# A perceiver block on one core: six of eight softmax normalisations on GpSimd, the output product in two halves of heads, and routing one-hots made one strip earlier

## The reference, cut to what matters

```python
x = x + xattn(layernorm(x), ctx, ctx)     # x: 64 x 64 x 256, ctx: 64 x 256 x 256
x = x + attn(layernorm(x))                # self attention with rotary positions
out = x + ffn(layernorm(x))               # shared expert, and top 2 of 8 routed experts

def xattn(query, key, value):             # 16 heads of 64
    q, k, v = query @ Wq + bq, key @ Wk + bk, value @ Wv + bv
    attn = softmax(q k^T / 8)             # per batch and head 64 x 256
    out = (attn v) @ Wo + bo + query      # 1024 -> 256
    return (out - mean) * rsqrt(var + 1e-5) * gamma + beta
```

## Time and profile before

| | us |
|---|---|
| three timed runs | 2184.82, 2184.95, 2186.15 |
| their median | 2184.95 |
| the profiled execution | 2187.32 |
| span of its trace (first to last instruction) | 2185.6 |
| PE busy | 2117.3 |
| DVE busy | 1609.6 |
| ACT busy | 1280.6 |
| POOL busy | 675.7 |
| cross attention | from the start to about 1407 |
| shared expert's sixteen strips with placing | 1717 to 1800 |

### The profile page before, as it was taken

One profiled execution on the slowest core, in us unless ns is written; L12 is line 12 of the kernel. 1 busy time (PEld: TensorE's weight loads), 2 busy tenths in 40 slices (PEclk: granted clock), 3 DMA queues, 4 the chain that ended last, 5 costly groups with the idle time before them and its releaser, 6 DMA issues.

```text
span 2185.6 us, 46111 instructions
## 1 busy us (share of the span) xinstructions
PE 2117.3 (97%) x15864; PEld 1855.5 (85%) x15865; DVE 1609.6 (74%) x3025; ACT 1280.6 (59%) x3067; POOL 675.7 (31%) x620
## 2 busy tenths in 40 slices
PE   8999999999999999999999999899998999999997
PEld 7898888888888888888888888677776888888886
DVE  6667768778777677687687786699996767666665
ACT  5556566556566565566565665477775335555553
POOL 4011011011010010110110101188885234777775
PEclk9999999999999999999999999999999999999999
DMA  4001010010010010010100100244433222333332
GB/s 153 10 21 34 0 34 24 10 34 19 14 34 19 15 34 14 19 32 2 34 24 10 34 10 1 63 153 153 151 121 100 87 78 51 54 55 53 53 55 42
DMA packets 100685, 103.90 MB, mean 48 GB/s; under 512 B 11952, under 2 KB 90160, under 8 KB 100624
## 3 DMA queue, kind: packets, MB, share of 16 engines
q1 hardware_dynamic: 86992, 84.47, 12.4%
q0 software_dynamic: 13632, 18.62, 5.2%
HBM read 72.52 MB, written 30.54 MB: 47 GB/s over the span
## 4 chain that ended last, share of the span: by engine, by line
PE 56%; DVE 17%; issue 10%; POOL 10%; ACT 4%; DMA 2%; DVEq 1%; POOLq 0%; SPq 0%; ACTq 0%
PE banks L906 29%; PE banks L949 5%; PE banks L991 5%; PE banks L1001 5%; POOL out_dram L2378 4%; PE banks L976 4%; POOL r_x L2342 3%; PE banks L2217 3%; DVE q_st L652 2%; POOL index L2349 2%; DVE s_peak L1535 2%; DVE s_rsum L1581 2%; ACT probs L541 2%; DVE z L846 1%; DMA out_dram<-r_y,index 1%
## 5 line engine op out<-in xcount | busy, mean ns | idle before, releaser
L906 PE MATMUL banks<-ctxT_hi,qk_hi 128*128 128x256 f32 x1024 | 300.5, 293 | 0.0
L906 PE MATMUL banks<-ctxT_hi,qk_lo 128*128 128x256 f32 x1024 | 289.5, 283 | 0.0
L906 PE MATMUL banks<-ctxT_lo,qk_hi 128*128 128x256 f32 x1024 | 288.4, 282 | 0.0
L541 ACT ACTIVATE probs<-banks,nbias 128x256 f32<-128x256 f32 x512 | 236.6, 485 | 71.6 <-DVE nbias L674 71.2
L548 ACT ACTIVATE pc<-banks 128x512 f32<-128x512 f32 x256 | 153.0, 598 | 191.3 <-PE banks L906 186.5
L632 DVE TENSOR_TENSOR qk_lo<-banks,qk_hi 128x512 fp32r<-128x512 f32 x256 | 165.8, 685 | 68.9 <-ACT qk_hi L503 68.8
L906 PE MATMUL banks<-pT_hi,ctx_hi 128*128 128x512 f32 x512 | 206.2, 403 | 4.7 <-DVE qk_lo L632 3.1
L432 POOL TENSOR_TENSOR rstd<-mv,power 128x2 f32<-128x2 f32 x32 | 22.2, 694 | 597.0 <-DVE mv L724 597.0
L632 DVE TENSOR_TENSOR pT_lo<-banks,pT_hi 128x512 fp32r<-128x512 f32 x256 | 164.6, 684 | 56.3 <-ACT pT_hi L503 55.7
L906 PE MATMUL banks<-pT_hi,ctx_lo 128*128 128x512 f32 x512 | 201.6, 394 | 0.0
L906 PE MATMUL banks<-pT_lo,ctx_hi 128*128 128x512 f32 x512 | 200.2, 391 | 0.0
(11 more groups left out here) (271 smaller groups left out, 6062.4 us busy)
## 6 DMA issues: line engine op xcount, KB each, us to landing
ctx_raw<-in_ctx_dram SPq DMA_DIRECT2D x64, 256.0 KB, 2.7
experts_w<-in_L_ffn_We_dram SPq DMA_DIRECT2D x24, 512.0 KB, 4.0
x_in<-in_x_dram SPq DMA_DIRECT2D x16, 256.0 KB, 2.8
x_again<-in_x_dram SPq DMA_DIRECT2D x16, 256.0 KB, 2.9
x_stream<-z SPq DMA_DIRECT2D x16, 256.0 KB, 2.2
s_x<-x_stream SPq DMA_DIRECT2D x32, 128.0 KB, 3.7
s_x_again<-x_stream SPq DMA_DIRECT2D x32, 128.0 KB, 2.1
x_normalised<-s_xl SPq DMA_DIRECT2D x32, 128.0 KB, 1.7
```

The source lines that it names most:

```text
L541: nc.scalar.activation(probs[:, s % 2, p, :], scores[:, s % 2, p // 2, (p % 2) * SK:(p % 2 + 1) * SK], ACT.Exp, bias=nbias[:, s % 2, p:p + ...
L906: last = nc.tensor.matmul(out, a, b, start=(n == 0), stop=(n == 3 * len(pairs) - 1))
```

## The change

Three edits.

1. Normalising of steps 1 to 6 moves to GpSimd: a power of -1 of the four sums (`rinv`), then the product of 128x1024. Steps 0 and 7 stay on DVE. GpSimd's program is rewritten by steps, and the context tiles 2 and 3 are now split in steps 0 and 1 of the group that uses them, behind the normalising of step 1 for the last one.
2. The output product is made by halves of the heads instead of by tiles. The bank of half 1 (four pairs, both tiles) is made in step 7 of the same group and added to `resid`; that of half 0 in step 3 of the next, and added to give `z`. The number of matmuls is the same: eight in each bank. In step 3 the first `do_pc` bank comes behind the second fold instead of the fourth. In step 7 DVE does `peaks` first, then `ctx_lower`.
3. `spread_out` is done one strip earlier.

```diff
-def part_of_pc(half, i):
-    c = i - (1 if half else 2)
+def part_of_pc(i):
+    c = i - 1
...
-                if s == 3 and g.prev and i < TILES:
-                    out.append(("o", i))
+                if i == 0 and (g.cur if half else g.prev):
+                    out.append(("o", half))
...
+        def normalise(g, s):                       # GpSimd
+            pool.wait_ge(exp_done, PAIRS * (STEPS * g.at + s + 1))
+            pool.sem_inc(pool_past, 1)
+            nc.gpsimd.tensor_tensor(rinv[:, s % 2, :], rsum[:, s % 2, :], inverse[:, :], ALU.pow).then_inc(rinv_done, 1)
+            pool.wait_ge(rinv_done, len(POOL_STEPS) * g.at + s)
+            pool.sem_inc(pool_past, 1)
+            nc.gpsimd.tensor_tensor(probs[:, s % 2], probs[:, s % 2],
+                                    rinv[:, s % 2, :].unsqueeze(2).broadcast_to([P, PAIRS, SK]),
+                                    ALU.mult).then_inc(probs_pool, 1)
...
+            for s in range(STEPS):
+                if s == 4 and g.prev:
+                    rsqrt(g, 1, tail_stats, tail_rstd, g.at)
+                if s == 4 and g.next:
+                    rsqrt(g, 0, ln_stats, ln_rstd, g.at + 2)
+                if s in POOL_STEPS:                # 1 to 6
+                    normalise(g, s)
+                if s < 2 and g.prev:
+                    split_ctx(g, s + 2, -1)
+                if s >= 6 and g.next:
+                    split_ctx(g, s - 6)
...
+        def add_o(g, half, out):                   # DVE
+            bank, free = wait_filled(dve, g, ("o", half))
+            nc.vector.tensor_tensor(out[:, :, :], bank.rearrange("p (n d) -> p n d", n=TILES), resid[:, :, :],
+                                    ALU.add).then_inc(free, 1)
...
-                if s == STEPS - 1 and g.next:
-                    ctx_lower(g, b)
-                    for h in range(2):
-                        fold_lower(g, half, h)
                 if g.cur:
                     peaks(g, s)
-                if half == 1 and g.next and s < STEPS - 1:
+                if half == 1 and g.next:
                     ctx_lower(g, b)
...
-                if g.cur:
+                if g.cur and s not in POOL_STEPS:
                     normalise(g, s)
...
         def do_pT(g, s):
-            pe.wait_ge(probs_done, STEPS * g.at + s)
+            if s - 1 in POOL_STEPS:
+                pe.wait_ge(probs_pool, len(POOL_STEPS) * g.at + s - 1)
+            else:
+                pe.wait_ge(probs_done, 2 * g.at + s)
...
-        def do_o(g, n):
+        def do_o(g, half):
             for j in range(2):
-                wait_freed(pe, g, ("v", 0, j))
-            bank, done = bank_for(pe, g, ("o", n))
-            for m in range(HALF):
-                last = nc.tensor.matmul(bank[:, 0:D], oT[:, m, n * P:(n + 1) * P], wo[:, m, :],
-                                        start=(m == 0), stop=(m == HALF - 1))
+                wait_freed(pe, g, ("v", half, j))
+            bank, done = bank_for(pe, g, ("o", half))
+            first = (1 - half) * PAIRS
+            for n in range(TILES):
+                for m in range(first, first + PAIRS):
+                    last = nc.tensor.matmul(bank[:, n * D:(n + 1) * D], oT[:, m, n * P:(n + 1) * P], wo[:, m, :],
+                                            start=(m == first), stop=(m == first + PAIRS - 1))
             last.then_inc(done, 1)
...
-            if 0 <= i + 1 - PLACE_AT < BATCHES:
-                spread_out(i + 1 - PLACE_AT)
+            if 0 <= i + 2 - PLACE_AT < BATCHES:
+                spread_out(i + 2 - PLACE_AT)
```

More of the change, by code:

```diff
@@ L831, in vector @@
                 if b == 3:
-                    for i in range(half, HALF // 2):
-                        if s == 3 and g.prev and i < TILES:
-                            bank, free = wait_filled(dve, g, ("o", i))
-                            nc.vector.tensor_tensor(z[:, i, :], bank[:, 0:D], resid[:, i, :], ALU.add).then_inc(free, 1)
+                    for i in range(HALF // 2):
+                        if s == 7 and g.cur and i == 0:
+                            dve.wait_ge(resid_done, g.at + 1)
+                            add_o(g, half, resid)
+                        if s == 3 and g.prev and i == 0:
+                            wait_freed(dve, g, ("o", 1), -1)
+                            add_o(g, half, z)
                         if s == 7 and g.next and i == 3:
```

60 lines of the change are left out of this document (23 added, 37 removed).

## The result

| | before | after |
|---|---|---|
| median of the runs, us | 2184.89 (2184.11 to 2186.15, 4 runs) | 2171.73 (2170.11 to 2173.67, 4 runs) |
| span of the profiled execution, us | 2185.6 | 2170.1 |
| granted clock of TensorE | 0.994 | 0.993 |

The ratio is 0.9936, with a 95% interval of 0.9924 to 0.9949: faster by 0.51 to 0.76%. The forecast was 2169.0 us, which is 15.9 us less; measured are 13.2 us less.

What follows compares the result with a forecast made beforehand. Only TensorE was full, so the change could give only its stalls. Terms summed to -16.0 us: 2187.3 to 2171.3 us for the profiled execution, 2169.0 for the median (2.4 lower); own range 2163 to 2176.

Steps and rivals of the forecast that it cites:

- placing: Sixteen placings and the wait before the first: with one-hots a strip earlier the losses go, -4.8 us, bounds -5.2 and -3.
- the block: DVE operations reading two SBUF tiles wait for GpSimd's product; `top` in steps 2, 5 and 6 takes 1 to 1.5 us.
- step 6: Step 6 of a group: `nbias` and `xT_lower` half a microsecond later, just in time; 0.05 x 15 = +0.8 us.
- first and last group: First group: -0.9 at the wait for DVE's first fold, +0.3 in step 2; last group's moved output product costs the same.
- step 7, folds: TensorE's 0.9 us lost at step 7's folds all goes behind the output product; -0.9 x 15 = -13.5 us.
- step 3, folds: Folds 4 to 7 in a row make TensorE wait at the last two banks; 0.38 x 15 = +5.7 us.
- step 5, transposes: Second bank of transposes gets back 0.33 of 0.59 us lost, since `top` waits for POOL's product; -5.0 us.
- step 2, exponentials: `top` held up, exponentials 0.8 us later, queries and second transposes bank 0.1 late; 14 groups, +1.4 us.
- `nbias` behind cast and subtraction: Rival: in step 2 POOL's cast and subtraction both precede `nbias`, 1.4 us instead of 0.1; 2187 us, chance 0.11.
- the slow neighbour: Rival: POOL's product takes 2427 ns instead of 1907, delaying steps 2, 5 and 6; 2190.5 us, chance 0.12.
- No block: Rival: small operations slip in, step 5 gives 0.59 us, steps 2 and 6 cost nothing; 2163 us, chance 0.14.
- Stalls elsewhere: Rival: the six losses of 0.1 us return in the new order, step 7 gains only 0.29; 2178 us, chance 0.13.

Runs made afterwards that it cites:

- halves_dve: The changed kernel with all eight normalisations of a group on DVE, new order kept; 2170.63 us, ratio 0.9938 to the kernel before.
- pc_apart: The changed kernel with step 3's two `do_pc` banks behind the folds of slots 0 and 2 instead of 0 and 1; 2170.55 us, ratio 0.9942.
- output_between: The changed kernel with step 3's output half between the folds of slots 0 and 1, `do_pc` behind slots 1 and 2; 2172.17 us, ratio 0.9939.
- nbias_on_act: The changed kernel with the exponentials' bias made by ScalarE, VectorE left with the maximum alone; 2163.57 us, ratio 0.9902.
- act_all: act_rec4 plus the step 3 order of output_between; 2160.50 us, ratio 0.9885.
- act_rec4: nbias_on_act plus, in step 4 alone, the reciprocal on DVE behind the residual additions; 2157.99 us, ratio 0.9872.

## Why the prediction was right, point by point

The time was 2.7 us off. The mechanisms held where the large terms are: the losses that go in step 7 and at the placings, the block in steps 2 and 5, the new loss in step 3. The small terms (step 6, first and last group) did not come as put, and the placings are right in sum with some luck, as told below. Between the spans of the two profiled executions lie 15.5 us, close to the 16.0 of the sum; that is luck too, since 4.0 of them are in the start, which is not the change's. The medians differ by 13.2: the profiled execution lay 2.4 us above the median before and 0.1 above it after. The measured terms are read from the steps:

| term | predicted | measured | by |
|---|---|---|---|
| step 7, folds | -13.5 | -13.0 | -(13.15 - 15.60 + 3.38), x 14 |
| step 3, folds | +5.7 | +5.0 | 14.20 - 13.87, x 15 |
| step 5, transposes | -5.0 | -3.0 | 7.57 - 7.37, x 15 |
| step 2, exponentials | +1.4 | +1.0 | 0.07 x 14 |
| step 6 | +0.8 | 0 | 14.17 both |
| placing | -4.8 | -4.8 | 3.65 in the periods, 1.17 before the first |
| first group, but its step 5 | -0.6 | 0.0 | steps 2, 3 and 7: +0.36 - 0.43 + 0.10 |
| last group, steps 4 and 5 | 0 | +0.5 | 6.56 + 6.96 against 6.50 + 6.50 |
| sum | -16.0 | -14.3 | |

*Step 7.* Right for a group, wrong by one in their number: the first group's step 7 took 12.12 us before and had no such loss. The losses before and inside the folds are gone (the earlier trace rows against the rows above). With `halves_dve` at 15.57 us the cause is the 3.4 us of output product that now cover the drain of the context bank, and not the normalising taken off DVE: that version has all of it on DVE and the same step 7. It also has the new order on DVE, the maxima ahead of the context tile, and no run takes the two apart; that order alone has DVE free the bank later and not sooner.

*Step 3.* Right in size (0.33 for 0.38) and in place, the banks freed by DVE behind ScalarE. I had put it at the last two banks: TensorE loses 0.24 us ahead of the transposes (743.08 to 743.44, where 0.12 are due) and 0.13 inside them; and `pc_apart` and `output_between` show that it moves with the run of folds rather than going.

*Step 5.* The block is as predicted, `top` ended by the product, and with 1.66 us a little longer than the 1 to 1.5 put for it. What failed in size is the end of the product. From the first scores of step 5 (760.39 before, 751.30 after) the power was to begin at 2.87 us and the product to end at 5.92; they do at 2.98 and 6.05. The power takes 1008 ns and not 918, which I had extended from one and two columns, and it begins 0.11 later. `nbias` and `ctx_lower` move by the same 0.13 us: 0.20 gained instead of 0.33, -3.0 instead of -5.0 us.

*Step 2.* Right to the order of the three on POOL: `nbias` gets in behind the cast, and ACT's 0.62 us of idle time are used up. Only in the first group does the block count in full, 1.6 us (see `nbias_on_act`). It is here that two rivals part: `nbias` behind cast and subtraction would have been 18 us.

*Step 6.* `top` is held up there too (763.08, 1.56 us), and the 0.05 us that I had put for it do not appear: the step takes 14.17 us as before.

*Placing.* Right in sum, by luck, and not in its parts. An undisturbed period is 4.71 us in the profile after and not 4.83, which gives 1.8 us more over fifteen, and 1.7 are lost again: three of the fifteen hold new stalls, of 0.28, 0.44 and 0.44 us, at the second product of the strip, and two more last about 0.1 longer. DVE's `f_h_lo`, of two SBUF inputs, lies under POOL's `f_by_tile` (1735.76, 2.10 us) there and takes 1.43 us:

```profile
1736.99 1.43 DVE L2191 TENSOR_TENSOR f_h_lo<-f_h,f_h_hi 128x512 fp32r<-128x512 f32 x1 [0.70 <-ACT f_h_hi L2003]
...
1738.86 0.19 PEld L2252 LDWEIGHTS banks<-f_w_hi,f_h_hi 128*128 128x128 f32 x1 [0.52 <-DVE f_h_lo L2191]
```

I had not looked for the block there.

*First and last group.* In the first, the wait for DVE's fold falls to 2.05 us from 3.07, which is the 0.9 put for it, but step 3 as a whole gains 0.43 and step 2 loses 0.36 where 0.3 was put. Behind that wait TensorE's granted clock is low in both kernels, 0.76 over 64.08 to 71.17 us before and 0.75 over 60.37 to 67.13 after, and the sum had no term for it. In the last group step 5 has no context tile, and TensorE comes to GpSimd's product before it is done. I had left that group out. Timeline of PE:

```profile
1349.57 1.09 PE L988 MATMUL banks<-ident,probs 128*128 128x128 f32 x8 [0.20 <-POOL probs L439]
```

*The rivals.* POOL's product is 1894 ns, not 2427: the slow neighbour falls, by the earlier trace rows and the row above. No block falls by `top` at 1.66 us. Stalls elsewhere is right for one place only, step 3, which was in the sum.

*Not in the sum.* The stretches in which nothing was changed differ between kernels. Up to the first transposes it is 36.6 to 41.0 us, and from the last output product to the first placing 316.5 to 320.9 over the thirteen kernels profiled here; each is one execution. For `act_all` against `act_rec4` the medians show it too. The records of that pair tell where the second kind lies. From 1402 to 1630 us of `act_rec4` the granted clock is 1.00 in both, and `act_all` loses 2.7 us: every second pass of self attention's loop lasts 8.08 us there against 7.85, from one product of GpSimd to the next (7.98 in the changed kernel, 7.89 before). The rest, about 1.2 us, is lost ahead of that stretch and behind it, where TensorE's clock falls to its lower level at times; over the 32 us from 1630 the granted clock is 0.89 in `act_rec4` and 0.84 in `act_all` at the same place. Why the same code settles at another period is open. So a sum from one loop is good to about 2 us here, and the verdict on each term above rests on the step times, which repeat within 0.12 us from group to group, and within 0.06 for steps 1 to 6.

## What to carry to other kernels

Before work goes to GpSimd, list what VectorE does while it runs: an operation that reads two tiles of SBUF, however small, lasted here until GpSimd's product had ended, so did a `tensor_scalar` of four columns, and all that is queued behind it on VectorE waits too. Put GpSimd's operation where VectorE evicts PSUM, and give the small dependent operations to ScalarE. Count such a block also where it meets nothing that covers it, as in the first group: the stall can bring TensorE's clock down behind it. And when a stall is removed by a long product put ahead of it, look at what that product covered where it stood before.

## What the runs showed of the hardware

- An operation on VectorE of 128x4 with a single SBUF input (`tensor_scalar`) took 1.67 us under GpSimd's product of 128x1024, as one with two inputs did (1.66); unhindered, `top` takes 0.16. The maxima (1.23 us) and an eviction with one PSUM and one SBUF input (0.68 us) kept their time, and in self attention so did batch norm statistics of 128x256 (0.41 us) and a `tensor_scalar` of 128x1 (0.15 us) under other operations of GpSimd.
- GpSimd's power takes 582 ns on average for one column (median 559), 694 to 698 for two and 1008 for four, so the straight line through the first two averages, 918, was too low. It did not hold VectorE up: in the last group of the changed kernel `z` (L860, 128x256, two SBUF inputs) took 0.48 us from 1358.88 on under a power that ran from 1358.78 for 1.01 us.
- Between two operations of GpSimd that follow without a wait, VectorE's waiting operation gets in: `top` ended at 722.87 with the product (722.84), and `nbias` at 723.42 with the cast (723.40), ahead of the subtraction (723.48).
- After the wait in step 2 of the first group TensorE ran the next 3.4 us at a granted clock of 0.50 in the changed kernel (transposes 2.58 us after the matmul before them) and at 1.00 with the bias on ScalarE (0.95 us).
